# Where the last batch of projections issues the row loads of unit 1 and the first values

## The chip, the cores and the metric

The kernel runs on one core of a Trainium2 chip. The metric is the device time of one launch in microseconds, as the median over runs. The engines are TensorE (PE in the profile), VectorE (DVE), ScalarE (ACT), GpSimd (POOL) and SyncE (SP), which here issues nearly all DMAs. Each engine takes its instructions in program order, and semaphores order the engines among each other.

## The reference, cut to what matters

The reference is a residual attention block followed by a residual quaternion rotation, on x of 8 batches x 512 tokens x 512 features:

```
q, k, v = x @ Wq.T, x @ Wk.T, x @ Wv.T          # 16 heads of 32 features
scores  = q @ k.T * 32**-0.5                    # 512 x 512 per head
scores  = where(mask, -inf, scores)
out     = softmax(scores) @ v  -> @ Wo.T
x       = x + rmsnorm(out) * rms_scale * (1 + sc) + shift   # sc, shift from silu(cond) @ Wc.T + bc
x       = x + rotation of x by normalised quaternions (a 512 x 512 structure of 4 x 4 diagonal blocks)
```

All sums are float32. A projection is made of three matmul passes over float32r halves (hi*hi, hi*lo, lo*hi).

## The kernel before, in words

The program has two parts that overlap at their border.

**Projections** (`projections`, lines 161 to 580). They run over batches 0 to 7. For one batch TensorE works through 4 tasks of V, 4 tasks of Q and 4 tasks of K (`batch` at L476, `passes` at L466, whose matmuls are L471 to L473); one task is 12 matmuls of 128x512 into one of four PSUM banks. In the last batch the V tasks are left out and made later, in the attention part (`held_values`, L831). So the last batch is Q0, Q1, Q2, Q3, K0, K1, K2, K3. After each Q or K task ScalarE copies the bank to `late[:, g]` (the hi half, L337) and VectorE writes the difference to `late[:, 4 + g]` (the lo half, L400), where g is the task's number in its group of four. SyncE then stores both halves to DRAM scratch: `store_qk`, L267, with one DMA of 256 KB at L270 and one at L271. The same four places of `late` serve Q and K: before ScalarE copies K of group g into place g, it waits at L336 until both stores of Q of group g have landed (`qk_stored[g]`). VectorE comes next on the same bank, and the bank is what TensorE writes four tasks later.

**Attention** (`attention`, from L583). It runs over 32 units of 4 heads, four units to a batch; unit u has 16 score tiles (4 heads x 4 chunks of 128 queries), numbered n in `ORDER`. A score tile is one matmul, L120 in `Scores.score`. VectorE adds the mask and takes the minimum (L129 in `mask`), ScalarE takes the exponential (L137), TensorE transposes the tile (L788), ScalarE or VectorE moves it out of PSUM (L1013, L901), and one unit later TensorE multiplies with the values (L816). Three PSUM banks hold scores, so score n waits for mask n - 3 (L119). TensorE writes score n + 7 ahead of the transposes of tile n.

A unit's scores need its **rows**: `q_rows` and `k_rows`, each 4 DMAs of 256 KB that write 32 partitions from scratch (`load_q` L85, with its DMA at L86, and `load_k` L89, L90). There are two places for rows, u % 2. The first score of a unit waits for all eight DMAs of the unit (L113 to L117). The first score of unit 1 is n = 16, which TensorE takes ahead of the transposes of tile n = 9.

**The border.** The first nine score tiles of unit 0 are computed inside the last batch (`EARLY`, L26): tiles 0 to 2 behind K0, 3 to 5 behind K1, 6 to 8 behind K2, each with its masks directly behind the L400 instruction of the same task on VectorE. The rows of units 0 and 1 belong to batch 0, so their scratch was written long before; the places they go to in SBUF are free once `x` of the last batch has been split (`x_lo_ready`, waited for at L289).

SyncE issues in program order (`batch` at L273 to L302): in batch 6 (`unit=0`) the rows of unit 0, two DMAs behind each pair of K stores; at the start of batch 7 (`unit=1`) all eight DMAs of the rows of unit 1 in the place where other batches store V; then the Q stores, then the values of batch 0 (`v_sb`, one DMA of 1 MB, L296), then the K stores. After that SyncE waits for all stores (L743) and for score n = 15 (L710), and loads the rows of unit 2.

Of the kernel before, what the change touches and what calls it, by code (L numbers as in the profile page):

```python
# [18 lines left out]
TC = S // P  # L19
HG = P // D  # L20
NG = H // HG
# [46 lines left out]
def f32(ap):  # L68

    return ap.bitcast(F32)  # L70
# [90 lines left out]
def projections(nc, held, block, banks, xT, wT, scr, raw, setup, rows, scores, late, kept, done, wo_hi, wo_lo, mask,  # L161
# [4 lines left out]
    with ExitStack() as ctx:  # L166
# [68 lines left out]
        @block.sync  # L235
        def _(sp):
            def load_x(b, p):
                sp.dma_start(x_raw[p], xT[b].rearrange("(k p) t -> p k t", p=P)).then_inc(x_in[p], 16)

            def load_w(n):  # L240
                sp.dma_start(w_raw[n % 2], wT[W_ORDER[n]].rearrange("(k p) e -> p k e", p=P)).then_inc(w_in[n % 2], 16)

            for k in range(KC):
                sp.dma_start(w_raw[0][:, k], wT[W_ORDER[0]][k * P:(k + 1) * P, :]).then_inc(first_w_in[k], 16)
                if k > 0:
                    sp.dma_start(x_raw[0][:, k], xT[0, k * P:(k + 1) * P, :]).then_inc(first_x_in[k], 16)
            for k in range(KC):
                sp.dma_start(w_raw[1][:, k], wT[W_ORDER[1]][k * P:(k + 1) * P, :]).then_inc(second_w_in[k], 16)
            sp.wait_ge(first_lo, 2 * KC)
            load_w(2)  # L250
            sp.dma_start(mask_words[:, :, :], mask.rearrange("(c p) t -> p c t", p=P)).then_inc(loaded, 16)
            sp.dma_start(cT[:, :], condT).then_inc(loaded, 16)
            sp.dma_start(quat[:, 0:8, :], cond.partition_broadcast(P)).then_inc(loaded, 16)
            sp.dma_start(quat[:, 8:12, :], q_right.partition_broadcast(P)).then_inc(loaded, 16)
            sp.dma_start(gate_b[:, :], gate.partition_broadcast(P)).then_inc(loaded, 16)
            sp.dma_start(wc[:, :], wcT).then_inc(loaded, 16)
            sp.dma_start(bc8[:, :], bc.partition_broadcast(B)).then_inc(loaded, 16)
            sp.dma_start(rms8[:, :], rms_scale.partition_broadcast(B)).then_inc(loaded, 16)
            load_x(1, 1)
            sp.wait_ge(second_lo, KC)  # L260
            load_w(3)

            def store_v(b, c):
                sp.wait_ge(v_copied, VT * b + c + 1)
                sp.dma_start(scr["v"][b, c], v_out[:, c, :]).then_inc(v_stored[c], 16)

            def store_qk(b, which, g):  # L267
                sp.wait_ge(qk_lo_ready, QKT * b + NG * which + g + 1)
                to = scr["qk"[which]][b * NG + g]
                sp.dma_start(to[0], late[:, g, :]).then_inc(qk_stored[g], 16)  # L270
                sp.dma_start(to[1], late[:, 4 + g, :]).then_inc(qk_stored[g], 16)  # L271

            def batch(b, p, more, unit=None):  # L273
                for c in range(TC):
                    if unit != 1:
                        store_v(b, c)
                    else:
                        rows.load_q(sp, 1, c)
                        rows.load_k(sp, 1, c)
                if more:  # L280
                    if not (isinstance(b, int) and b == 0):
                        sp.wait_ge(x_lo_ready, b)
                    load_x(b + 2, p)
                for which in range(2):
                    if unit == 0 and which == 1:
                        sp.wait_ge(mod_ready, 1)
                        sp.dma_start(mod_scr, mod[:, :]).then_inc(mod_stored, 16)
                        sp.wait_ge(rot_ready, 1)
                        sp.wait_ge(x_lo_ready, B - 1)  # L289
                        for g in range(2):  # L290
                            sp.wait_ge(qk_stored[g], 64)
                    if unit == 1 and which == 1:
                        for c in range(TC):
                            sp.wait_ge(v_stored[c], 16 * (B - 1))
                        sp.wait_ge(projected, TASKS * b + NG)
                        sp.dma_start(f32(kept.values[:, 0]), scr["v"][0].rearrange("c p e -> p c e")).then_inc(  # L296
                            kept.v_in[0], 16)
                    for g in range(NG):
                        store_qk(b, which, g)
                        if unit == 0 and which == 1:  # L300
                            rows.load_q(sp, 0, g)
                            rows.load_k(sp, 0, g)  # L302

            batch(0, 0, True)
            batch(1, 1, True)
            with sp.Fori(2, B - 3, 2) as b:
                batch(b, 0, True)
                batch(b + 1, 1, True)
            batch(B - 2, 0, False, unit=0)
            batch(B - 1, 1, False, unit=1)  # L310
# [932 lines left out]
```

## Time and profile before

| | us |
|---|---|
| median of 3 runs (lowest to highest) | 865.63 (865.63 to 866.34) |
| the profiled execution, time | 866.87 |
| its span, first to last instruction | 865.1 |
| mean granted TensorE clock of the span | 0.995 |
| PE busy | 850.7 (98%) |
| DVE, ACT, POOL busy | 629.5, 616.0, 482.6 |

The profiled execution has 1.77 us outside its span. Granted clock is a share of TensorE's 2.4 GHz: 1.00 is 2.4 GHz and 0.50 is 1.2 GHz. The span falls into projections (to about 270 us) and attention (from there to the end). A wait is put down to the semaphore that came last.

### The profile page before, as it was taken

The page shows a single profiled execution, that of the slowest core. Times are in us where ns is not written, and L with a number is a line of the kernel's source. Part 1 is how long each engine was busy: PE and PEld are TensorE (multiplying, and loading weights), DVE is VectorE, ACT ScalarE, POOL GpSimd, SP SyncE. Part 2 cuts the span into 40 slices and gives each one's busy share as a digit, 9 for nine tenths or more (in the row PEclk, how much of TensorE's full clock was granted, in tenths as well). Part 3 has the DMA queues.
Part 4 walks back from the last instruction along what each step waited for, and adds up shares of the span by engine and source line. Part 5 has one row for each costly group of instructions (what it writes and reads, how often), then busy time and mean ns, then how long its engine had stood idle before and what let it go on. Part 6 is the DMA issues. An engine that isn't in the chain of part 4 may idle for free.

```text
span 865.1 us, 17179 instructions
## 1 busy us (share of the span) xinstructions
PE 850.7 (98%) x5344; PEld 642.7 (74%) x5344; DVE 629.5 (73%) x1524; ACT 616.0 (71%) x1504; POOL 482.6 (56%) x346
## 2 busy tenths in 40 slices
PE   9999999999979999999999999999999999999997
PEld 6788888888867767776777767777677767777774
DVE  4521321322327889999899998999999998999886
ACT  6232332332317889999999999999999999999882
POOL 0999990000000112477577766777667775777794
PEclk9999999999998999999999999999999999999999
DMA  8954644644695667687766777578767778669201
GB/s 285 343 204 167 224 170 182 230 178 174 207 282 197 146 145 192 151 210 158 180 174 149 161 180 195 124 183 210 164 152 179 163 161 196 157 146 235 84 25 50
DMA packets 82355, 153.76 MB, mean 178 GB/s; under 512 B 8520, under 2 KB 9160, under 8 KB 82272
## 3 DMA queue, kind: packets, MB, share of 16 engines
q1 hardware_dynamic: 82128, 152.49, 65.0%
q8 instruction: 40, 0.66, 0.3%
q14 instruction: 43, 0.35, 0.2%
q10 hardware_dynamic: 144, 0.26, 0.1%
HBM read 102.35 MB, written 50.36 MB: 177 GB/s over the span
## 4 chain that ended last, share of the span: by engine, by line
PE 94%; DMA 1%; DVE 1%; SPq 1%; issue 1%; ACT 1%; POOL 0%; DVEq 0%; ACTq 0%
PE banks L788 26%; PE banks L120 14%; PE banks L816 13%; PE banks L851 10%; PE banks L471 9%; PE banks L472 9%; PE banks L473 9%; PE banks L797 2%; DMA q_scratch<-late 1%; PE banks L831 1%; PE banks L456 1%; PE banks L444 1%; SPq L90 0%; SPq L86 0%; DVE probs L685 0%
## 5 line engine op out<-in xcount | busy, mean ns | idle before, releaser
L137 ACT ACTIVATE probs<-probs,least 128x512 f32<-128x512 f32 x512 | 363.3, 713 | 0.1
L129 DVE CUSTOM_DVE_ANT_0 probs<-banks,mask_bias 128x512 f32<-128x512 f32 x512 | 330.4, 683 | 37.6 <-PE banks L120 37.6
L788 PE MATMUL banks<-ident,probs 128*128 128x128 f32 x2048 | 306.4, 272 | 0.7 <-DVE turned_probs L901 0.6
L788 PEld LDWEIGHTS banks<-ident,probs 128*128 128x128 f32 x2048 | 252.3, 140 | 56.8 <-ACT probs L137 1.8
L120 PE MATMUL banks<-k_rows,q_rows 128*128 128x512 f32 x496 | 237.4, 481 | 5.6 <-DVE least L129 5.6
L901 DVE COPY turned_probs<-banks 128x512 f32<-128x512 f32 x256 | 175.8, 687 | 2.3 <-PE banks L788 2.3
L400 DVE SCALAR_TENSOR_TENSOR late<-banks,late 128x512 fp32r<-128x512 f32 x64 | 43.9, 690 | 167.0 <-ACT late L337 166.8
L1013 ACT ACTIVATE turned_probs<-banks 128x512 f32<-128x512 f32 x256 | 147.1, 587 | 16.9 <-PE banks L788 13.6
L337 ACT ACTIVATE late<-banks 128x512 fp32r<-128x512 f32 x64 | 38.2, 598 | 128.1 <-PE banks L473 112.3
L685 POOL TENSOR_TENSOR late<-rot,late 128x2048 f32<-128x2048 f32 x28 | 129.3, 4619 | 0.0
L816 PE MATMUL banks<-turned_probs,v_sb 128*32 128x512 f32 (+1 forms) x1088 | 116.9, 570 | 1.3 <-ACT turned_probs L1013 1.3
L120 PEld LDWEIGHTS banks<-k_rows,q_rows 128*128 128x128 f32 x496 | 94.4, 190 | 10.3 <-DVE least L129 6.6
L137 ACT ACTIVATION_READ_ACCUMULATOR probs<-probs,least 128x1 f32 x512 | 97.5, 190 | 0.0
L1102 POOL CAST o_hi<-o_T 128x512 fp32r<-128x512 f32 x29 | 17.8, 613 | 140.4 <-DVE o_T L911 112.3
L816 PEld LDWEIGHTS banks<-turned_probs,v_sb 128*32 128x32 f32 x1088 | 32.1, 109 | 63.0 <-issue 55.4
L1152 POOL MEMSET minus_half<- 128x1 f32 x1 | 0.1, 99 | 140.0 <-PE banks L788 140.0
L1147 POOL TENSOR_TENSOR late<-late 128x1024 f32<-128x1024 f32 x29 | 69.6, 2399 | 2.2
L330 ACT ACTIVATE v_out<-banks 128x512 f32<-128x512 f32 x28 | 16.7, 598 | 55.9 <-PE banks L473 53.0
L471 PE MATMUL banks<-o_hi,w_hi_k 128*128 128x512 f32 x128 | 50.7, 396 | 0.0
L851 PE MATMUL banks<-wo_hi,o_hi 128*128 128x512 f32 x128 | 50.7, 396 | 0.0
L472 PE MATMUL banks<-o_lo,w_hi_k 128*128 128x512 f32 x128 | 50.7, 396 | 0.0
L473 PE MATMUL banks<-o_hi,w_lo_k 128*128 128x512 f32 x128 | 50.5, 395 | 0.0
(134 smaller groups left out, 1269.3 us busy)
## 6 DMA issues: line engine op xcount, KB each, us to landing
q_rows<-q_scratch SPq DMA_DIRECT2D x128, 256.0 KB, 6.0
k_rows<-k_scratch SPq DMA_DIRECT2D x124, 256.0 KB, 6.6
q_scratch<-late SPq DMA_DIRECT2D x64, 256.0 KB, 2.4
k_scratch<-late SPq DMA_DIRECT2D x64, 256.0 KB, 2.3
v_sb<-v_scratch SPq DMA_DIRECT2D x8, 1024.0 KB, 11.6
out<-late SPq DMA_DIRECT2D x29, 256.0 KB, 7.3
raw<-in_xT SPq DMA_DIRECT2D x7, 1024.0 KB, 5.6
v_scratch<-v_out SPq DMA_DIRECT2D x28, 256.0 KB, 2.0
```

The costliest lines, as they stand in the source:

```text
L120: pe.matmul(self.ps[:, n % SCORE_BANKS, :], self.rows.q[:, u % 2, i, c * P:(c + 1) * P], self.rows.k_of(u)[:, i, :], start=True, stop=True ...
L129: dve.tensor_tensor_reduce(self.probs[:, n % RING, :], self.ps[:, n % SCORE_BANKS, :], self.mask_bias[:, c, :], 1.0, 3e38, ALU.add, ALU.mi ...
L137: act.activation(self.probs[:, n % RING, :], self.probs[:, n % RING, :], ACT.Exp, bias=self.least[:, n % 32:n % 32 + 1], scale=-1.0, accum ...
L471: pe.matmul(out, hi(k), other_hi(k), start=(k == 0), stop=False)
L472: pe.matmul(out, hi(k), other_lo(k), start=False, stop=False)
L473: last = pe.matmul(out, lo(k), other_hi(k), start=False, stop=(k == KC - 1))
L685: return eng.tensor_tensor(to.rearrange("p j (i d) -> p j i d", i=4), rot[:, :, :, :], chunk.rearrange("p (j d) -> p j d", j=4).unsqueeze( ...
L788: last = pe.transpose(turn_bank("tile", n)[:, j * P:(j + 1) * P], probs[:, n % RING, j * P:(j + 1) * P], ident[:, :])
L816: last = pe.matmul(value_ps[i * D:(i + 1) * D, cols], v_sb[:, b % 2, part, h * D:(h + 1) * D], turned_probs[:, (HG * u + i) % SLOTS, part, ...
L851: last = pe.matmul(y_of(m), left[:, b % 2, k, t], right[:, k, :], start=(part == 0), stop=(part == 11))
L901: dve.tensor_copy(turned_probs[:, h % SLOTS, :, c * P:(c + 1) * P], turn_bank("tile", n).rearrange("p (j t) -> p j t", j=TC)).then_inc(out ...
L1013: act.activation(turned_probs[:, h % SLOTS, :, c * P:(c + 1) * P], turn_bank("tile", n).rearrange("p (j t) -> p j t", j=TC), ACT.Copy).the ...
```

## The change

SyncE's program of the last batch is written in another order. The eight row loads of unit 1 leave the start of the batch, and two of them (q and k) stand behind each pair of K stores, as those of unit 0 do in the batch before. The load of the first values moves from ahead of the K stores to behind all of them and their rows. No instruction is added or removed, and no wait changes its condition. On the other engines nothing is moved.

```
             def batch(b, p, more, unit=None):
-                for c in range(TC):
-                    if unit != 1:
-                        store_v(b, c)
-                    else:
-                        rows.load_q(sp, 1, c)
-                        rows.load_k(sp, 1, c)
+                for c in range(TC) if unit != 1 else ():
+                    store_v(b, c)
...
+                    for g in range(NG):
+                        store_qk(b, which, g)
+                        if unit is not None and which == 1:
+                            rows.load_q(sp, unit, g)
+                            rows.load_k(sp, unit, g)
                     if unit == 1 and which == 1:
                         for c in range(TC):
                             sp.wait_ge(v_stored[c], 16 * (B - 1))
                         sp.wait_ge(projected, TASKS * b + NG)
                         sp.dma_start(f32(kept.values[:, 0]), scr["v"][0].rearrange("c p e -> p c e")).then_inc(
                             kept.v_in[0], 16)
-                    for g in range(NG):
-                        store_qk(b, which, g)
-                        if unit == 0 and which == 1:
-                            rows.load_q(sp, 0, g)
-                            rows.load_k(sp, 0, g)
```

The first place is the border of batches 6 and 7 on SyncE. Before, from the last two row loads of unit 0 to the stores of Q0:

```order
L86 DMA q_rows<-q_scratch 32x4x512
L90 DMA k_rows<-k_scratch 32x4x512
L86 DMA q_rows<-q_scratch 32x4x512
L90 DMA k_rows<-k_scratch 32x4x512
L86 DMA q_rows<-q_scratch 32x4x512
L90 DMA k_rows<-k_scratch 32x4x512
L86 DMA q_rows<-q_scratch 32x4x512
L90 DMA k_rows<-k_scratch 32x4x512
L86 DMA q_rows<-q_scratch 32x4x512
L90 DMA k_rows<-k_scratch 32x4x512
L270 DMA q_scratch<-late 128x512 [waits qk_lo_ready]
L271 DMA q_scratch<-late 128x512
```

Of these the first two are unit 0's, the next eight unit 1's. The same place in the changed kernel:

```order
L86 DMA q_rows<-q_scratch 32x4x512
L90 DMA k_rows<-k_scratch 32x4x512
L270 DMA q_scratch<-late 128x512 [waits qk_lo_ready]
L271 DMA q_scratch<-late 128x512
L270 DMA q_scratch<-late 128x512 [waits qk_lo_ready]
L271 DMA q_scratch<-late 128x512
```

The stores of Q0 now follow unit 0's last rows directly.

The second place is the end of batch 7 on SyncE, with the stores of K. Before, from the stores of Q3 to those of K1:

```order
L270 DMA q_scratch<-late 128x512 [waits qk_lo_ready]
L271 DMA q_scratch<-late 128x512
L296 DMA v_sb<-v_scratch 128x4x512 [waits v_stored3,v_stored2,projected,v_stored1,v_stored0]
L270 DMA k_scratch<-late 128x512 [waits qk_lo_ready]
L271 DMA k_scratch<-late 128x512
L270 DMA k_scratch<-late 128x512 [waits qk_lo_ready]
L271 DMA k_scratch<-late 128x512
```

In the changed kernel, from the stores of K2 to the values:

```order
L270 DMA k_scratch<-late 128x512 [waits qk_lo_ready]
L271 DMA k_scratch<-late 128x512
L86 DMA q_rows<-q_scratch 32x4x512
L90 DMA k_rows<-k_scratch 32x4x512
L270 DMA k_scratch<-late 128x512 [waits qk_lo_ready]
L271 DMA k_scratch<-late 128x512
L86 DMA q_rows<-q_scratch 32x4x512
L90 DMA k_rows<-k_scratch 32x4x512
L297 DMA v_sb<-v_scratch 128x4x512 [waits v_stored3,v_stored2,projected,v_stored1,v_stored0]
```

Each pair of K stores is followed by one q and one k row load of unit 1, and the values stand last, directly ahead of the attention part's first wait.

## Rows read from the trace of the kernel before

**Rows 1.** The page, part 1: busy time and share of the span.
```profile
PE 850.7 (98%) x5344; PEld 642.7 (74%) x5344; DVE 629.5 (73%) x1524; ACT 616.0 (71%) x1504; POOL 482.6 (56%) x346
```
**Rows 2.** Chain of waits, 215 to 300 us: start, duration, what.
```profile
239.92 0.75 SPq L90
240.71 0.51 SPq L86
...
244.18 0.43 SPq L90
...
245.13 12.15 DMA q_scratch<-late
...
283.99 3.64 PE banks L816 x32
```
**Rows 3.** Timeline of ACT, 218 to 290 us: start, duration, instruction, [idle before].
```profile
239.53 0.60 ACT L337 ACTIVATE late<-banks 128x512 fp32r<-128x512 f32 x1 [2.12 <-PE banks L473]
...
257.36 0.60 ACT L337 ACTIVATE late<-banks 128x512 fp32r<-128x512 f32 x1 [9.07 <-DMA q_scratch<-late]
...
266.28 0.60 ACT L337 ACTIVATE late<-banks 128x512 fp32r<-128x512 f32 x1 [4.73 <-PE banks L473]
```
**Rows 4.** Timeline of PE, 248 to 286 us, and its L120 at 294.73.
```profile
250.21 0.84 PE L120 MATMUL banks<-k_rows,q_rows 128*128 128x512 f32 x3
250.89 0.39 PE L471 MATMUL banks<-o_hi,w_hi_k 128*128 128x512 f32 x1
...
259.34 2.02 PE L120 MATMUL banks<-k_rows,q_rows 128*128 128x512 f32 x3 [5.57 <-DVE least L129]
...
266.08 0.84 PE L120 MATMUL banks<-k_rows,q_rows 128*128 128x512 f32 x3
...
269.49 1.04 PE L788 MATMUL banks<-ident,probs 128*128 128x128 f32 x8
...
276.78 0.48 PE L120 MATMUL banks<-k_rows,q_rows 128*128 128x512 f32 x1
...
294.73 0.48 PE L120 MATMUL banks<-k_rows,q_rows 128*128 128x512 f32 x1
```
**Rows 5.** Stretches: engines' busy time (x instructions), PEclk, DMA share, GB/s.
```profile
260.00:265.00 5.00, 5.00 (x12) 3.71 (x12) 2.94 (x9) 1.55 (x6) 0.00 (x0) 0.50 1.04 402
...
270.00:275.00 5.00, 4.91 (x33) 3.81 (x32) 4.69 (x11) 5.00 (x14) 0.10 (x1) 1.00 0.28 105
```
**Rows 6.** Timeline of DVE, 218 to 290 us.
```profile
260.43 0.69 DVE L400 SCALAR_TENSOR_TENSOR late<-banks,late 128x512 fp32r<-128x512 f32 x1
...
262.25 0.69 DVE L129 CUSTOM_DVE_ANT_0 probs<-banks,mask_bias 128x512 f32<-128x512 f32 x1
```
**Rows 7.** Timeline of SP's queue, 229 to 260 us: the issues of DMAs.
```profile
230.14 0.34 SPq L270 DMA_DIRECT2D k_scratch<-late  x1
...
231.50 0.45 SPq L90 DMA_DIRECT2D k_rows<-k_scratch  x1
...
249.41 0.44 SPq L271 DMA_DIRECT2D q_scratch<-late  x1
250.02 0.39 SPq L296 DMA_DIRECT2D v_sb<-v_scratch  x1
258.71 0.33 SPq L270 DMA_DIRECT2D k_scratch<-late  x1
```
**Rows 8.** DMA issued at 231.50: size, us from issue to landing.
```profile
k_rows<-k_scratch SPq DMA_DIRECT2D x1, 256.0 KB, 4.1
```
**Rows 9.** DMA issued at 239.92, the last row load of unit 0.
```profile
k_rows<-k_scratch SPq DMA_DIRECT2D x1, 256.0 KB, 6.5
```
**Rows 10.** DMA issued at 244.18, the last row load of unit 1.
```profile
k_rows<-k_scratch SPq DMA_DIRECT2D x1, 256.0 KB, 11.9
```
**Rows 11.** DMA issued at 249.41, the second store of Q3.
```profile
q_scratch<-late SPq DMA_DIRECT2D x1, 256.0 KB, 11.8
```
**Rows 12.** DMA issued at 250.02, the first values.
```profile
v_sb<-v_scratch SPq DMA_DIRECT2D x1, 1024.0 KB, 13.6
```

## The prediction

> **What bounds the kernel now.** I read the busy times first: PE is busy for 98% of the span, so only places where PE stands still, or runs at a lower clock, are worth looking for [rows 1]. Next the chain of waits around the change. From 239.92 us on it is a run of DMA issues on SyncE, and then one DMA, the second store of Q0, which takes 12.15 us from its issue at 245.13 to its landing at 257.28 [rows 2]. The timeline of ACT says who stood there: the copy of K0 starts at 257.36 after 9.07 us idle, released by that store [rows 3]. It needs the place in `late` that the store reads. The timeline of PE then shows the price. The three scores that follow K1 start at 259.34 after 5.57 us without work, put down to L129 on DVE [rows 4]. These are masks 0 to 2, queued on DVE behind the lo half of K0, which itself waits for ACT. So the chain is: row loads of unit 1, store of Q0, copy of K0, its lo half, mask, score.
>
> How long PE lost there follows from the slots. Three scores take 250.89 - 250.21 = 0.68 us at full clock, and from the scores at 266.08 to the transposes at 269.49 (three scores and the 12 matmuls of K3) are 3.41 us, so a K task takes 2.73 [rows 4]. K1 starts at 250.89 and its slot ends at 253.62. Scores 3 to 5 start at 259.34: 5.72 us lost. From there to 266.08 is 6.74 us for work (three scores and K2) that takes 3.41 afterwards: 3.33 us lost to the clock. The stretches show it: granted clock 0.50 (the 1.2 GHz level) in 260 to 265, after the stand of 5.57 us, and 1.00 (2.4 GHz) in 270 to 275 [rows 5].
>
> **The wait that goes.** SyncE issues unit 1's eight row loads from 240.71 on, the last at 244.18 [rows 2]. Q0's copy on ACT is at 239.53 [rows 3]. From a copy to the issue of its first store pass 258.71 - 257.36 = 1.35 us [rows 3, 7], so Q0's store could be issued at 240.9. Being issued late cost it about 4 us. The larger part is the queue. The last row load of unit 0 is issued at 239.92 and lands after 6.5 us, at 246.4 [rows 2, 9]; the last one of unit 1, issued at 244.18, lands after 11.9 us, at 256.1 [rows 2, 10]. Eight row loads took 9.7 us, 1.21 us each. The last of the eight Q stores is issued at 249.41 and lands after 11.8, at 261.2 [rows 7, 11]: 5.1 us for eight, 0.64 each. Unit 1's loads and the stores thus came out in the order of issue.
>
> In the changed kernel Q0's two stores stand behind unit 0's rows only: 246.4 + 2 x 0.64 = 247.7. K0's copy can start 0.20 us behind PE's last matmul of the task (266.28 against 266.08 [rows 3, 4]), so at 250.21 + 0.20 = 250.41. It waits for nothing, with 2.7 us to spare. Q1 to Q3 are issued one task apart (2.7 us) and need 1.3 us of queue each, so they land well ahead of K1 to K3.
>
> What would be late next on that stretch is the mask. DVE starts K0's lo half some 0.6 us behind ACT, and from the start of K1's lo half (260.43) to the end of mask 5 (262.25 + 0.69) pass 2.51 us [rows 6]. K1's copy on ACT comes at 253.6 + 0.2 = 253.8, its lo half at 254.4, mask 5 ends at 256.9. Scores 6 to 8 start at 253.62 + 0.68 + 2.73 = 257.0. There PE has little over, but nothing is missing. So the transposes that start at 269.49 start at 257.0 + 3.41 = 260.4. The gain is 5.72 + 3.33 = 9.05 us up to here.
>
> **The wait that comes.** Unit 1's rows now compete with its own first score, n = 16, at 276.78 in this trace, 7.29 us behind the transposes [rows 4]. In the changed kernel PE asks for them at 260.4 + 7.3 = 267.7. When do they land? The pattern is in the trace, since batch 6 writes K stores and rows of unit 0 in just that order. Group 0 begins with the store at 230.14, its k row load is issued at 231.50 and lands after 4.1, at 235.6: 5.46 us for a group on a short queue [rows 7, 8]. Group 3's k row load lands at 246.4 [rows 9], so three further groups take 10.8 us, 3.60 each. (The sum of the parts, 2 x 0.64 + 2 x 1.21, gives 3.70.) In batch 7 SyncE can issue a group each 3.41 us (a K task and three scores), a little faster than the queue serves it. Group 0's store is issued at 250.41 + 1.35 = 251.8; last landing 251.8 + 5.46 + 10.8 = 268.0. Lower bound, if the queue kept pace with the issues: 251.8 + 3 x 3.41 + 5.46 = 267.5, no wait at all. Upper bound: the last row load, issued 3 x 3.41 + 1.36 us behind that store, at 263.4, with the 11.9 us of the longest row load [rows 10], 275.3. I take 268.0, since the 3.60 comes from the same instructions in the same order, and so a wait of 0.3 us.
>
> The Trainium skill, "DMA: Bandwidth & Descriptors", section "Where 436 GB/s comes from", has a port limit of 435 GB/s for 16 ports; an estimate from that page alone is 0.60 us for a row load. By it the queue would keep pace, the rows would land at the lower bound, and the gain would be 9.05 instead of 8.75. The trace has 1.21 us for these loads of 32 partitions, so I do not use it.
>
> **The rest of the edit.** The values are now issued behind all rows, at about 264. In the trace they are issued at 250.02 and land after 13.6 us, at 263.6, which is 2.4 us behind the last Q store [rows 7, 11, 12]. Behind the rows that is 268.0 + 2.4 = 270.4. PE uses them first at 283.99 [rows 2], or 274.9 with the 9.05 taken off: 4.5 us cover; if they came later than that, PE would wait by the difference. Queued behind them on SyncE are the wait for the K stores (L743) and the rows of unit 2, issued once score 15 is done, at about 267.5. K3's stores are issued at 262.0 behind group 2's rows (251.8 + 5.46 + 7.2 = 264.5) and land by 265.8, so that wait is not the last. Unit 2's eight loads are then served from 270.4 to 280.1. Its first score is at 294.73 [rows 4], then 285.7: 5.6 us cover. Everything on the other engines keeps its order and its distance to PE, and behind the border PE is the bound, so the shift is kept to the end.
>
> **The sum.** 9.05 - 0.3 = 8.75. The profiled execution of 866.87 us (span 865.1 and 1.77 around it) would become 858.1, its span 856.4. That execution lies 1.24 above the median shown, 865.63, from which I forecast 865.63 - 8.75, so 856.9 us.
>
> **The rivals.**
> *Rows late by several us.* The same mechanism as the 0.3, but SyncE or the queue is slower than in batch 6, with a landing at 269 to 273 instead of 268.0. For it: the queue is saturated in both cases, and unit 1's loads had 11.9 us [rows 10]. Against it: each group has 0.7 us more time than in batch 6. Price 1.3 to 5.3 us: 857.9 to 861.9.
> *The wait for Q0 stays in part.* If the backlog is not gone by 247.7, say the store still takes the 12.15 us from its new issue at 241.3, it lands at 253.5 and K0 is 3.1 us late. Mask 5's slack to scores 6 to 8 is small, and scores 3 to 5 stand 0.5 us behind their masks, so PE stands for about 2.6 us, probably with no fall of the clock. Gain 6.2 instead of 8.75: 859.5.
> *The landing order is not the issue order.* If Q0's stores could overtake rows ahead of them, moving the rows would gain only the delay of their issue, 245.13 - 241.3, some 3.8 us: 861.8. The Trainium skill, "DMA: Bandwidth & Descriptors", section "Queues, rings and completion order", says that completion is not first in, first out for one issuing engine. The trace speaks against it with 12.15 us for a 256 KB store behind the rows [rows 2], and landings at 246.4, 256.1, 257.3 and 261.2 in the order of issue.
> *Slower than before.* The stand moves from K1 to score 16. If the rows land near their upper bound, 275.3, PE stands from 267.7 for 7.6 us, and after a stand of this length the clock falls again, which cost 3.33 us here [rows 5]. Together 10.9 against 9.05 gained: 867.5. It decides from a landing at 267.7 + 5.7 = 273.4 on. Against it: the 11.9 us came from a queue of eight loads and eight stores at one time, here the loads enter it two at a time, a task apart.
>
> **Chances.** The forecast (a wait of 0 to 1.2 us, 856.6 to 857.8) 0.72; rows late 0.13; Q0 in part 0.06; order of landing 0.03; slower 0.03; something I have not seen 0.03. The range must leave out no more than 2 in 10: 855.9 to 860.6. Its lower end allows for the 0.7 us between the lowest and the highest of the runs shown. From no change a measurement can tell about 0.2% (1.7 us). Faster by more: 0.95; within: 0.02; slower: 0.03.
>
> **What would show it.** Right: ACT's copy of K0 near 250.4 and without a DMA as releaser; scores 3 to 5 near 253.6; clock 1.00 from 250 to 270; first transposes near 260.4; a PE wait at the score of unit 1 below about 1 us, with a row load as releaser; span near 856.4. Wrong: a stand of PE near 267.7 of several us (rows late), an ACT wait on q_scratch (queue not empty), or a PE wait for v_sb near 275.

## The result, and the profile after

| | before | changed |
|---|---|---|
| median of 5 runs, us | 865.63 (865.52 to 866.34) | 858.04 (857.55 to 858.58) |
| ratio, 95% interval | | 0.9908 (0.9894 to 0.9921) |
| profiled execution, us | 866.87 | 858.58 |
| its span | 865.1 | 856.8 |
| mean granted clock | 0.995 | 1.000 |

The changed kernel is 7.6 us faster by the medians and 8.3 us by the two profiled executions. In the changed kernel the lines of `attention` stand 4 lower: L784 is the transpose that was L788, L812 the values that were L816, L333 the copy that was L337.

The timeline of ACT (start, duration, instruction, idle before it) answers to [rows 3]:

```profile
239.73 0.60 ACT L333 ACTIVATE late<-banks 128x512 fp32r<-128x512 f32 x1 [2.12 <-PE banks L469]
...
250.61 0.60 ACT L333 ACTIVATE late<-banks 128x512 fp32r<-128x512 f32 x1 [2.12 <-PE banks L469]
254.01 0.60 ACT L333 ACTIVATE late<-banks 128x512 fp32r<-128x512 f32 x1 [2.80 <-PE banks L469]
```

The row at 239.73 is the copy of Q0, 0.20 us later than before, which is a difference in when the executions reach this point. K0's copy is at 250.61, and its releaser is PE, no longer a DMA. It came at 257.36 before.

The timeline of PE answers to [rows 4]:

```profile
250.41 0.84 PE L120 MATMUL banks<-k_rows,q_rows 128*128 128x512 f32 x3
...
253.81 0.84 PE L120 MATMUL banks<-k_rows,q_rows 128*128 128x512 f32 x3
...
257.21 0.84 PE L120 MATMUL banks<-k_rows,q_rows 128*128 128x512 f32 x3
...
260.62 1.04 PE L784 MATMUL banks<-ident,probs 128*128 128x128 f32 x8
...
268.68 0.47 PE L120 MATMUL banks<-k_rows,q_rows 128*128 128x512 f32 x1 [0.53 <-issue]
```

Each group of three scores follows the one before by 3.40 us, with nothing between the tasks. The transposes start at 260.62 instead of 269.49. Score 16 at 268.68 has a new idle time of 0.53 us. "issue" means that the profile has no releaser for it. The landings show which it was: SyncE's timeline has the last row load of unit 1 at 263.55, and the DMA view gives 5.0 us to its landing, so 268.55, 0.13 us ahead of the score.

```profile
241.49 0.43 SPq L271 DMA_DIRECT2D q_scratch<-late  x1
...
263.55 0.46 SPq L90 DMA_DIRECT2D k_rows<-k_scratch  x1
264.17 0.39 SPq L297 DMA_DIRECT2D v_sb<-v_scratch  x1
267.59 0.31 SPq L86 DMA_DIRECT2D q_rows<-q_scratch  x1
```

The three DMAs from 241.49, 263.55 and 264.17, size and us from issue to landing, each from the DMA view of the moment of its issue; they answer to [rows 9 to 12]:

```profile
q_scratch<-late SPq DMA_DIRECT2D x1, 256.0 KB, 6.4
...
k_rows<-k_scratch SPq DMA_DIRECT2D x1, 256.0 KB, 5.0
...
v_sb<-v_scratch SPq DMA_DIRECT2D x1, 1024.0 KB, 7.7
```

Q0's second store lands at 247.9 instead of 257.3. The values land at 271.9, 4.0 us ahead of their first use at 275.87.

The stretches (PE, PEld, DVE, ACT, POOL busy with instructions, granted clock, DMA share, GB/s) answer to [rows 5]:

```profile
255.00:260.00 5.00, 5.00 (x24) 4.14 (x23) 4.12 (x13) 4.31 (x13) 0.00 (x0) 1.00 1.05 276
260.00:265.00 5.00, 4.91 (x33) 3.82 (x32) 4.11 (x10) 4.30 (x12) 0.10 (x1) 1.00 1.04 316
265.00:270.00 5.00, 4.47 (x31) 3.71 (x29) 5.00 (x14) 4.13 (x13) 0.00 (x0) 1.00 1.04 290
```

The clock stays at 1.00. The only stretch in which PE lacks something is 265 to 270, which holds the wait for the rows.

### The profile page after: what moved, and what is told of

The parts are those of the page before. It is cut to its first block, busy times and chain, and to the rows that moved or that the text cites. A ratio compares the mean times of both kernels' runs of the same rounds, so it can differ in the third digit from the quotient of the medians.

```text
span 856.8 us, 17179 instructions
## 1 busy us (share of the span) xinstructions
PE 847.5 (99%) x5344; PEld 641.2 (75%) x5344; DVE 629.9 (74%) x1524; ACT 615.9 (72%) x1504; POOL 482.6 (56%) x346
## 4 chain that ended last, share of the span: by engine, by line
PE 97%; DVE 1%; ACT 1%; issue 1%; POOL 0%; ACTq 0%; DVEq 0%
PE banks L784 26%; PE banks L120 14%; PE banks L812 13%; PE banks L847 10%; PE banks L467 9%; PE banks L468 9%; PE banks L469 9%; PE banks L793 2%; PE banks L827 1%; PE banks L452 1%; PE banks L440 1%; ACT probs L137 0%; DVE probs L681 0%; ACT turned_probs L1009 0%; PE banks L506 0%
## 5 line engine op out<-in xcount | busy, mean ns | idle before, releaser
L784 PE MATMUL banks<-ident,probs 128*128 128x128 f32 x2048 | 306.4, 272 | 0.7 <-ACT probs L137 0.6
L784 PEld LDWEIGHTS banks<-ident,probs 128*128 128x128 f32 x2048 | 252.4, 140 | 56.5 <-ACT probs L137 1.8
L120 PE MATMUL banks<-k_rows,q_rows 128*128 128x512 f32 x496 | 236.1, 478 | 0.5 <-issue 0.5
L333 ACT ACTIVATE late<-banks 128x512 fp32r<-128x512 f32 x64 | 38.2, 598 | 119.3 <-PE banks L469 113.0
L812 PE MATMUL banks<-turned_probs,v_sb 128*32 128x512 f32 (+1 forms) x1088 | 117.0, 570 | 1.3 <-ACT turned_probs L1009 1.3
L120 PEld LDWEIGHTS banks<-k_rows,q_rows 128*128 128x128 f32 x496 | 94.1, 190 | 4.3 <-issue 0.7
L812 PEld LDWEIGHTS banks<-turned_probs,v_sb 128*32 128x32 f32 x1088 | 32.1, 109 | 63.0 <-issue 55.4
L847 PE MATMUL banks<-wo_hi,o_lo 128*128 128x512 f32 x128 | 50.6, 395 | 0.0
L847 PE MATMUL banks<-wo_lo,o_hi 128*128 128x512 f32 x128 | 50.5, 394 | 0.0
```

The lines of the kernel that those rows point to most:

```text
L120: pe.matmul(self.ps[:, n % SCORE_BANKS, :], self.rows.q[:, u % 2, i, c * P:(c + 1) * P], self.rows.k_of(u)[:, i, :], start=True, stop=True ...
L784: last = pe.transpose(turn_bank("tile", n)[:, j * P:(j + 1) * P], probs[:, n % RING, j * P:(j + 1) * P], ident[:, :])
L812: last = pe.matmul(value_ps[i * D:(i + 1) * D, cols], v_sb[:, b % 2, part, h * D:(h + 1) * D], turned_probs[:, (HG * u + i) % SLOTS, part, ...
L847: last = pe.matmul(y_of(m), left[:, b % 2, k, t], right[:, k, :], start=(part == 0), stop=(part == 11))
```

## The experiments

Executions differ by up to 1.1 us before the border is reached (the copy of Q0 comes between 238.82 and 239.93), so the profiles are compared by the distance from that copy to the first matmul with values (L816 or its counterpart). A stand is a time in which PE has no work, read as the idle time in its timeline.

| kernel | row loads of unit 1 ahead of Q0's stores | PE idle, us (at score 3, at 16) | distance, us | median of runs, us |
|---|---|---|---|---|
| before | 8 | 5.57, 0 | 44.46 | 865.63 (865.52 to 866.34) |
| changed | 0 | 0, 0.53 | 36.14 | 858.04 (857.55 to 858.58) |
| changed, again | 0 | 0, 0.51 | 36.15 | 858.10 (858.00 to 859.06) |
| e1 rows alone | 0 | 0, 3.03 | 38.68 | 862.75 (861.20 to 863.97) |
| e2 values alone | 8 | 5.57, 0 | 43.66 | 865.79 (865.25 to 866.88) |
| e3 Q stores on ACT's queue | 8, in another queue | 0, 0 | 36.19 | 858.44 (857.72 to 858.50) |
| e4 four ahead | 4 | 0.92, 0 | 37.43 | 859.13 (858.45 to 859.62) |
| e5 all behind | 0 | 0, 6.90 | 44.61 | 867.50 (865.98 to 869.52) |
| e6 behind Q1 to K0 | 0 | 0, 0 | 35.41 | 857.77 (857.11 to 858.04) |
| e7 six ahead | 6 | 3.38, 0 | 41.47 | 863.72 (862.45 to 864.87) |

The kernel before had 866.16 beside e1 to e4 and 866.04 beside the others. The ratios to it, with 95% intervals: e1 0.9963 (0.9951 to 0.9976), e2 0.9999 (0.9990 to 1.0007), e3 0.9913 (0.9898 to 0.9927), e4 0.9918 (0.9906 to 0.9931), e5 1.0021 (1.0010 to 1.0032), e6 0.9906 (0.9889 to 0.9922), e7 0.9976 (0.9966 to 0.9985), changed again 0.9911 (0.9895 to 0.9928).

**e1: the rows moved, the values left in their place.** Against the changed kernel:

```
-  [values of batch 0 behind the loop over g]
+  [values of batch 0 ahead of the loop over g: between Q3's stores and K0's]
```

> The rows of unit 1 move behind the K stores as in the changed kernel; the first values stay ahead of the K stores. Theory (the queue serves in order of issue): Q0's stores are not held, so K0's copy starts at about 250.6 without a wait. The values, issued near 250.2, take 2.4 us of the queue just ahead of K0's stores, so the rows of unit 1 land about 1.9 us later than in the changed kernel (near 270.4 instead of 268.5) and PE waits 2.0 to 2.4 us at score 16 instead of 0.53. Median about 859.8. Rival (the place of the values is indifferent, as they fit into an idle queue): 858.0.

K0's copy is at 250.44 without a wait. The last row load (issued at 263.37, 7.6 us to landing) lands at 270.97, and PE's timeline has the wait:

```profile
271.04 0.47 PE L120 MATMUL banks<-k_rows,q_rows 128*128 128x512 f32 x1 [3.03 <-issue]
```

The mechanism is the one expected and its size was put too low. Counted from Q0's copy, the last row load lands 2.6 us later than in the changed kernel, where 1.9 had been expected, so the queue makes up for little of the values' time. The stand is 3.03 us, where 2.0 to 2.4 had been expected, and the median is 4.7 us above the changed kernel's instead of 1.8; the profiled execution (861.74) shows 3.2 of it. The second half of the edit is thus what makes the first half worth its full amount. The rival, that the place of the values is indifferent, falls. What the rest of the 4.7 us is stands under e8 and e9.

**e2: the values moved, the rows left in their place.** Against the kernel before:

```
-  [values ahead of the loop over g]
+  [values behind the loop over g]
```

> Only the first values move, behind the K stores; the rows of unit 1 stay at the start of the last batch. Theory: Q0's second store still takes about 12 us, K0's copy still starts near 257.4, PE stands for 5.6 us and the clock falls; the median is that of the kernel before, 865.6 within 0.5. Rival (the 1 MB of values ahead of the K stores was part of what held the border): 863 to 864.

The timeline of ACT has K0's copy:

```profile
256.81 0.60 ACT L337 ACTIVATE late<-banks 128x512 fp32r<-128x512 f32 x1 [9.07 <-DMA q_scratch<-late]
```

The time does not move (ratio 0.9999), K0's copy waits 9.07 us and PE 5.57 us, both as before. By itself the values' place gains nothing. The rival falls.

**e3: the order of before, Q's stores from another queue.** Against the kernel before:

```
 act:  for m in range(QKT): ...
+          if last and 1 <= m <= NG:
+              act.wait_ge(qk_lo_ready, QKT * b + m)
+              act.dma_start(to[0], late[:, m - 1, :]).then_inc(qk_stored[m - 1], 16)
+              act.dma_start(to[1], late[:, 4 + m - 1, :]).then_inc(qk_stored[m - 1], 16)
 sp:   [no store_qk for Q in batch 7]
```

> SyncE's order of the kernel before, with the rows of unit 1 at the start of the last batch; only the eight Q stores of that batch are issued from ScalarE's DMA queue, one task behind their copy. Theory (Q0's stores waited for their place in a queue that is served in order, not for bandwidth): they land within about 3 us of their issue, K0's copy starts near 250.5 with no wait, the clock stays at 1.00, and as the rows land before 262, PE does not wait at score 16 either: median 857.5. Rival (2 MB of rows and the stores share the 16 DMA engines, whichever queue they are in): Q0's stores still land after 253 and the gain is 6 us or less, 859.5 or more.

Timeline of the queues and of ACT:

```profile
241.93 0.45 ACTq L343 DMA_DIRECT2D q_scratch<-late  x1
...
250.79 0.60 ACT L337 ACTIVATE late<-banks 128x512 fp32r<-128x512 f32 x1 [3.22 <-DMA q_scratch<-late]
```

The DMA view of the moment of that store:

```profile
q_scratch<-late ACTq DMA_DIRECT2D x1, 256.0 KB, 8.8
```

Both numbers were off. The store lands at 250.7, neither within 3 us of its issue nor after 253. Without rows ahead of it in its own queue it still shares the engines with them, and it takes 8.8 us, against 12.15 behind the rows and 6.4 in the changed kernel. K0's copy is thereby 1.1 us later than it could have been. The three scores behind K1 then take 1.60 us instead of 0.84, PE has next to no idle time (4.79 us busy of the 5 from 250 to 255), the clock is 0.999 over the span, and nothing waits at score 16. So the time is that of the changed kernel with the rows still in their old place, but by another sum: scores 6 to 8 come 0.8 us late, and the 0.76 us that the changed kernel waits at score 16 is not there.

The edit moves two things at once. The store is in another queue, and it is also issued at 241.93 instead of 245.13, since ScalarE does not have eight row loads to issue first. It lands 6.6 us earlier (250.7 instead of 257.3), of which 0.7 us is an earlier Q0 copy (238.82 instead of 239.53), and 3.2 us of earlier issue alone would not give the rest. The stretches from 245 to 250 of the kernel before and of e3 show what the second queue adds:

```profile
245.00:250.00 5.00, 5.00 (x24) 4.14 (x23) 1.38 (x2) 1.17 (x2) 0.00 (x0) 1.00 1.08 214
...
245.00:250.00 5.00, 5.00 (x24) 4.14 (x23) 1.27 (x2) 0.60 (x1) 0.00 (x0) 1.00 1.06 302
```

With only row loads being served, 214 GB/s move; with the Q stores beside them, 302, at the same DMA share (1.08 and 1.06). So it is mostly the place in the queue that held Q0, and the rest is what the two queues take from each other.

**e4 and e7: four and six of the eight loads ahead.** Against the changed kernel (n is 2 or 3 pairs):

```
             def batch(b, p, more, unit=None):
+                for r in range(n) if unit == 1 else ():
+                    rows.load_q(sp, 1, r)
+                    rows.load_k(sp, 1, r)
...
                         store_qk(b, which, g)
-                        if unit is not None and which == 1:
+                        r = g + n if unit == 1 else g
+                        if unit is not None and which == 1 and r < NG:
```

> Four of the eight row loads of unit 1 stay ahead of Q0's stores, the other four stand behind the stores of K0 and K1. Theory: each row load ahead costs 1.21 us of queue, so Q0's second store lands near 246.6 + 4 x 1.21 + 1.3 = 252.8, K0's copy is 2.0 to 2.3 us late, PE stands 1.3 to 1.8 us before scores 3 to 5, and the clock does not fall; the rows land early enough for score 16. Median 857.5 + 1.5 = 859.0. Rival (any stand costs the fall of the clock as well, 3.3 us): about 862.3.

> Six of the eight row loads stay ahead of Q0's stores, the last two stand behind K0's. Theory: Q0's second store lands 2.4 us later than with four ahead (252.15 there), K0's copy is at 254.6 or so, PE stands about 3.4 us before score 3; if the clock stays at 1.00 after a stand of this length the time is some 3.5 us above the changed kernel, and if it falls, some 6.5 us. Rival (the cost does not grow with the loads ahead of the store): the time of the run with four ahead, 1 us above the changed kernel.

The copy of K0 and PE's timeline of e4:

```profile
252.26 0.60 ACT L337 ACTIVATE late<-banks 128x512 fp32r<-128x512 f32 x1 [4.41 <-DMA q_scratch<-late]
...
254.25 1.73 PE L120 MATMUL banks<-k_rows,q_rows 128*128 128x512 f32 x3 [0.92 <-DVE least L129]
```

The same of e7:

```profile
254.75 0.60 ACT L337 ACTIVATE late<-banks 128x512 fp32r<-128x512 f32 x1 [6.88 <-DMA q_scratch<-late]
...
256.73 1.92 PE L120 MATMUL banks<-k_rows,q_rows 128*128 128x512 f32 x3 [3.38 <-DVE least L129]
```

Q0's second store lands at 247.9 with no row load of unit 1 ahead of it (changed kernel), at 252.15 with four, at 254.65 with six and at 257.3 with eight (kernel before). That is 9.4 us for eight loads or 1.18 each, near the 1.21 us of the sum; the single steps are 1.1, 1.25 and 1.3 a load, read from executions that reach Q0's copy up to 0.6 us apart. The cost grows with the loads ahead of the store, and the rival of e7 falls.

The median of e4, 859.13, lies at the 859.0 expected, but not by the sum expected. The stand is 0.92 us instead of 1.3 to 1.8, then the three scores spread over 1.73 us while they wait for their masks, so scores 6 to 8 come 2.0 us late, and the wait of 0.76 us at score 16 is gone. The stand of e7 is 3.4 us as expected, and the clock answers to it. The median is 5.6 us above the changed kernel's beside it, where 6.5 had been expected if the clock fell. The stretches of e7:

```profile
255.00:260.00 5.00, 3.06 (x7) 2.06 (x8) 4.62 (x13) 3.17 (x8) 0.00 (x0) 0.81 1.05 362
260.00:265.00 5.00, 5.00 (x20) 4.00 (x20) 1.87 (x6) 2.18 (x6) 0.00 (x0) 0.85 0.45 133
```

In e4 every stretch from 245 to 285 has 1.00. So the rival of e4, that any stand costs the clock, falls as well.

**e5: all rows behind the last K store.** Against the changed kernel:

```
                     for g in range(NG):
                         store_qk(b, which, g)
-                        [q and k row load of unit 1, pair g]
+                    for r in range(NG) if unit == 1 and which == 1 else ():
+                        rows.load_q(sp, 1, r)
+                        rows.load_k(sp, 1, r)
```

> All eight row loads of unit 1 stand behind K3's stores, the values behind them. Theory: no wait at K0; the rows land near 264.9 + 8 x 1.21 = 274.6, PE stands from 268.2 for 6.5 us at score 16, and after a stand longer than that of the kernel before the clock falls to 0.50 again and takes about 3.3 us more: 9 us above the changed kernel, no faster than the kernel before (865.5 to 867.5). Rival (a stand in the attention part is made up, as ScalarE and VectorE are behind PE there and catch up, and the clock keeps): 3 to 6 us above the changed kernel.

PE's timeline and the stretches behind the wait:

```profile
274.69 0.77 PE L120 MATMUL banks<-k_rows,q_rows 128*128 128x512 f32 x1 [6.90 <-issue]
```

```profile
270.00:275.00 5.00, 0.31 (x1) 0.34 (x2) 0.00 (x0) 0.00 (x0) 0.00 (x0) 0.73 1.06 236
275.00:280.00 5.00, 5.00 (x20) 4.01 (x20) 2.49 (x6) 2.96 (x8) 0.00 (x0) 0.59 1.08 284
```

The last row load (issued at 266.04, 8.6 us) lands at 274.6, as worked out. The stand is 6.9 us (6.5 expected), and the clock falls. The fall costs less than the 3.3 us expected: from score 16 to the first values pass 9.28 us (274.69 to 283.97) instead of 7.20 in e1 (271.04 to 278.24), where the clock keeps, so 2.1 us. The median, 867.50, is at the upper end of the 865.5 to 867.5 expected and 1.5 us above the kernel before beside it; four of the ten executions, with a mean clock of 0.993 or 0.994, took 868.9 to 869.5 us. All that was gained at K0 is lost again at score 16.

**e6: the rows between the Q stores.** Against the changed kernel, the pairs stand behind Q1, Q2, Q3 and K0 instead of K0 to K3:

```
                         store_qk(b, which, g)
+                        r = NG * which + g - 1
-                        if unit is not None and which == 1:
+                        if unit == 1 and 0 <= r < NG:
```

> The pairs of row loads of unit 1 stand behind the stores of Q1, Q2, Q3 and K0 instead of K0 to K3; the values last. Theory: the queue is idle part of the time between Q0's landing (247.7) and K0's store (252), Q2's and Q3's stores have 5 us to spare, and the last row load lands near 262.5, so PE waits neither for Q0 nor for the rows: 0.5 us below the changed kernel. Rival (a row load ahead of Q2 and Q3 holds K2's or K3's copy): an ACT wait on q_scratch appears at K2 or K3 and the time is 1 us or more above the changed kernel.

SyncE's timeline and the DMA view of the last row load:

```profile
253.17 0.45 SPq L90 DMA_DIRECT2D k_rows<-k_scratch  x1
```

```profile
k_rows<-k_scratch SPq DMA_DIRECT2D x1, 256.0 KB, 8.4
```

It lands at 261.6, no copy of K waits for a store, and score 16 starts 7.31 us behind the transposes, as in the kernel before. The distance is 0.74 us shorter than in the changed kernel. In the medians it is 0.33 us (857.77 against 858.10 on the same chip), and the runs of the two overlap, so these medians do not tell it from nothing; that e6 is the fastest is shown by the profiles only.

**e8, e9 and e10: the spread of e1 and e7.** No edit; one more execution with a profile each.

> The kernel with the rows alone moved once more, for one profile: its times spread over 861.2 to 864.0, while its one profiled execution (861.7) had clock 1.00 throughout and a stand of 3.0 us. Theory: the clock falls after the stand of 3.0 us in some executions and not in others, and costs up to 2.5 us where it falls; an execution of 863 us or more shows a stretch below 1.00 right behind the stand, one near 861.5 does not. Rival (the spread comes from the landing of the rows): the stand itself differs by 1 us or more and the clock stays at 1.00.

> As the run before it: a second profile of the same kernel, for the same two theories.

> The kernel with six row loads ahead of Q0's stores once more, for one profile; its times spread over 862.5 to 864.9, and the profiled execution (863.5) had a clock of 0.81 and 0.85 in two stretches of 5 us behind a stand of 3.4 us. Theory: the stand is the same again within 0.2 us, and the time goes with the length of the stretch at half clock. Rival: the stand differs and the clock stretch is the same.

| run | time | stand | distance | clock behind it |
|---|---|---|---|---|
| e1 | 861.74 | 3.03 | 38.68 | 1.00 |
| e8, same kernel | 860.83 | 2.93 | 38.58 | 1.00 |
| e9, same kernel | 863.98 | 4.11 | 41.35 | 0.50 for some 3 us |
| e7 | 863.51 | 3.38 | 41.47 | 0.81, 0.85 in 255 to 265 |
| e10, same kernel | 864.17 | 2.72 | 41.52 | 0.61, 0.71 in 255 to 265 |

Stretches of e9, from the last microsecond of the stand on:

```profile
271.00:272.00 1.00, 0.04 (x1) 0.07 (x1) 0.00 (x0) 0.00 (x0) 0.00 (x0) 1.00 0.94 213
272.00:273.00 1.00, 1.00 (x5) 0.80 (x6) 0.35 (x1) 0.00 (x0) 0.00 (x0) 0.71 1.06 231
273.00:274.00 1.00, 1.00 (x5) 0.90 (x5) 0.35 (x2) 0.35 (x1) 0.00 (x0) 0.50 1.08 209
274.00:275.00 1.00, 1.00 (x5) 0.70 (x4) 0.70 (x2) 1.00 (x4) 0.00 (x0) 0.50 1.07 201
275.00:276.00 1.00, 1.00 (x6) 0.87 (x5) 0.21 (x1) 1.00 (x3) 0.00 (x0) 0.58 1.08 246
```

In e9 both theories hold a part: the stand is 1.1 us longer and the clock falls, together 2.7 us of distance against e1; the clock's part is 1.6. The rows of e9 lose their time in the last group only. The last landings of its four groups (two K stores with their two row loads each) are at 260.65, 264.05, 267.55 and 271.87, those of e1 at 260.37, 263.82, 267.36 and 270.97. Why this one step takes 4.3 us instead of 3.6 is open.

The median of e1 (862.75) lies 1 us above its first profiled execution, and the mean clock that is on record for every execution says why. Of the six executions of e1, those at 861.20 and 861.74 have a mean clock of 1.000, and those at 862.56, 862.93, 863.51 and 863.97 have 0.997 or 0.998. So the clock falls in four of six, and with e8 and e9 in five of eight. The ten executions of e7 split the same way: 862.45 to 863.51 at 0.997 or 0.998, 863.93 to 864.87 at 0.995.

For e10, its timeline and its stretches:

```profile
256.73 2.02 PE L120 MATMUL banks<-k_rows,q_rows 128*128 128x512 f32 x3 [2.72 <-DVE least L129]
```

```profile
255.00:260.00 5.00, 3.27 (x7) 2.24 (x8) 4.62 (x13) 3.17 (x8) 0.00 (x0) 0.61 0.96 327
260.00:265.00 5.00, 5.00 (x18) 3.93 (x17) 1.17 (x4) 1.47 (x4) 0.00 (x0) 0.71 0.46 134
```

A mean of 0.61 over 5 us is 3.9 us at 0.50, and 0.71 is 2.9, together 6.8 us at the lower clock; in e7 the 0.81 and 0.85 are 1.9 and 1.5, together 3.4. In e10 PE reached Q0's copy 0.67 us later than in e7 (239.77 and 239.10) while K0's copy came at the same 254.75, so the stand is 0.66 us shorter, and the clock costs 0.7 us more (scores 3 to 5 and K2 take 6.60 us instead of 5.89). The two parts cancel in the distance. The theory had expected the same stand. The clock's part does go with the time at half clock, the whole distance does not.

## Why the prediction was right

The measured 858.04 lies inside the stated range of 855.9 to 860.6, but outside the forecast's own band of 856.6 to 857.8. By the number it falls among the late rows (857.9 to 861.9), by the mechanism it does not: the wait is 0.76 us and the landing 268.55, where that rival has 269 to 273. What is missing lies in the sum, below.

**What bounds the kernel.** Right. The chain from row loads over Q0's store, K0's copy and the masks to the scores is shown from three sides: taking the rows away from the front of the store (changed kernel), giving the store another queue (e3), and changing the number of row loads ahead of it (e4, e7). One reading in the forecast was wrong without harm to it: that being issued late cost Q0's store about 4 us besides the queue. The landing moved by 9.4 us, and eight row loads at 1.21 us are 9.7, so the queue alone accounts for it.

**The wait that goes.** Forecast 9.05 us up to the first transposes. From Q0's copy to them it was 269.49 - 239.53 = 29.96 and is 260.62 - 239.73 = 20.89: 9.07. Q0's second store was put at 247.7 and landed at 247.9. K0's copy had 2.7 us to spare by the forecast and has it (250.61 against 247.9). The masks did not hold scores 6 to 8.

**The wait that comes.** Right in kind, too small in size. Forecast 0.3 us, measured 0.76: score 16 comes 8.06 us behind the transposes instead of 7.3 (0.53 of the 0.76 shows as idle time, the rest is the pipelined end of the work ahead). Two terms were off. One is the service of three groups, put at 10.8 us, or 3.60 each. The four groups' last landings in the changed kernel are at 257.4, 260.9, 264.5 and 268.55, so it was 11.1. The longest step is the last one here, 4.0 us; in the second profile of the changed kernel (257.6, 261.6, 265.1, 268.7) the sum is 11.1 again and the first step is the longest, 4.0. The other is the time from the landing to the score, 0.13 us, which the forecast left out.

**The rest of the edit.** The values landed 4.0 us ahead of their use (forecast 4.5). Behind the last row load they took 3.3 us instead of 2.4, so they landed at 271.9 instead of 270.4, and part of this is hidden because their use came later too (275.87 instead of 274.9). From there on the shift is kept: 8.32 us at the first values, 8.50 at the end of the span, both counted from Q0's copy. 0.20 us is given back by the later start.

**The sum against the medians.** The forecast was 8.75, the profiles gave 8.3 and the medians 7.6 and, beside e5 to e7, 7.9. The 0.46 us between forecast and profiles is the wait at score 16 (0.76 instead of 0.3), since the 0.20 us of the later start and the 0.18 us gained behind the border cancel. The rest, up to the medians, is put down to the clock: what it costs differs from one execution of the kernel before to the next. It cost 3.33 us in the profiled one. In e2, with the same stand of 5.57 us, scores and K2 take 264.70 - 258.79 = 5.91 us instead of 3.41, so the clock costs 2.50:

```profile
258.79 2.02 PE L120 MATMUL banks<-k_rows,q_rows 128*128 128x512 f32 x3 [5.57 <-DVE least L129]
...
264.70 0.84 PE L120 MATMUL banks<-k_rows,q_rows 128*128 128x512 f32 x3
```

The stretches say why the same stand costs less. Those of the kernel before that stand on either side of the 260 to 265 at 0.50 of [rows 5], then those of e2:

```profile
255.00:260.00 5.00, 0.66 (x2) 0.34 (x2) 2.01 (x6) 1.87 (x4) 0.00 (x0) 0.90 1.05 399
...
265.00:270.00 5.00, 5.00 (x24) 4.13 (x23) 2.52 (x7) 3.02 (x8) 0.00 (x0) 0.92 0.35 130
...
255.00:260.00 5.00, 1.21 (x2) 0.57 (x2) 2.56 (x8) 2.43 (x5) 0.00 (x0) 0.67 1.05 405
260.00:265.00 5.00, 5.00 (x16) 4.00 (x16) 2.39 (x7) 1.09 (x5) 0.00 (x0) 0.65 0.46 172
```

The time at 0.50 is equally long in both: 1.0 + 5.0 + 0.8 = 6.8 us and 3.3 + 3.5 = 6.8 us. But it begins at about 259.0 in the kernel before, 0.3 us ahead of the scores at 259.34, and at about 256.7 in e2, 2.1 us ahead of those at 258.79. The part that falls into the stand costs nothing.

5.72 + 2.50 - 0.76 is 7.5, and with 3.33 it is 8.3. The medians lie between. The time of the profiled execution of before, 866.87, was above all five runs of the table. Of the 36 other executions of the kernel before that ran beside e1 to e7, 33 have a mean clock of 0.995 or 0.996 and took 865.58 to 867.20 us, and three have 0.998 and took 864.28 to 864.90. Subtracting a gain that was read from one execution from a median of others overstated it by up to 0.8 us. How the clock's cost is spread over the executions without a profile is not shown.

**The rivals.** Rows late by several us did not come; e1 shows that it would have, had the values stayed ahead. Q0 held in part did not come; e4 is that case, at 1.3 us of distance over the changed kernel. The stand of about 2.6 us for which that rival expected no fall of the clock is near the 2.72 us of e10, where it fell. Landing out of the order of issue did not come: in the changed kernel, e1, e4, e6 and e7 the landings of Q's stores and unit 1's rows follow the order of issue, within the 0.1 us to which they are read. The slower case did not come either, but its mechanism and price are real: e5 puts the landing at 274.6, behind the 273.4 from which the forecast saw no gain, and is slower than before.

## What to carry to other kernels

Row loads that nobody needed for the next 27 us (issued from 240.7, needed near 267.7) cost 9 us here, because they stood just ahead of a small store that frees a buffer. Where the landings follow the order of issue, as in this queue, look at what is queued in front of each store that an engine waits for, and count its service time (here 1.21 us a row load). Place such loads where the queue has slack and the stores behind them have it too (e6, by its profile), and check the first user of the load in the same sum, since moving it too far (e5) gives everything back. When a profiled execution contains a stand with a fall of the clock, take the clock's part as a range over executions (1.6 to 3.3 us here), not as a term, and look at how much of the time at the lower clock lies inside the stand.

## What the runs showed of the hardware

A stand of PE does not decide by its length alone whether the granted clock falls. It stayed at 1.00 after stands of 0.53, 0.92, 2.93 and 3.03 us and fell with 2.72, 3.38, 4.11, 5.57 and 6.90 us. Not all of these are alike. The stands of 0.92, 2.72, 3.38 and 5.57 us lie before scores 3 to 5, and these three scores then took 1.73 to 2.02 us instead of 0.84; the others lie before score 16, with full work behind them. So that 2.72 us fell (e10) and 3.03 us did not (e1) compares two places. In one place and one kernel, the longer stand had the shorter time at the lower clock: 3.38 us with 3.4 us at 0.50 in e7, 2.72 us with 6.8 us in e10. And one kernel (e1, e8 and e9) kept a mean clock of 1.000 in three executions of eight and had 0.997 or 0.998 in five. The Trainium skill, "TensorE: Matmul & The Clock Gate", section "Part 1: The HAM clock gate (the "warmup" mystery)", says of the start of a kernel that the number of matmuls at the lower clock is "run-variable". These runs show such a variation at the fall of the clock in the middle of a kernel.

The same 6.8 us at the lower clock cost 3.33 us in the profiled execution of before and 2.50 in e2, by where it lay to the stand.

Two DMA queues issued from two engines share the DMA engines: the 256 KB store took 6.4 us behind unit 0's rows alone, 8.8 us in ScalarE's queue beside unit 1's rows (e3), and 12.15 us behind them. Eight row loads of 256 KB to 32 partitions took 9.7 us, 216 GB/s, and eight stores of 256 KB from 128 partitions 5.1 us, 410 GB/s, in the kernel before.
